# Contracting over 128 rows with zeros instead of 65 and 97, in the second layer's edge loop of a graph network on Trainium2

## The chip, the cores and the metric

The kernel runs on one core of one Trainium2 chip. The metric is the device time of one execution in microseconds (us); lower is better. Three executions of the kernel before are given, and one more was taken with the profiler, whose trace is what the rows below come from.

## What is computed

Two layers of an equivariant graph network on 12,500 nodes and 200,000 edges, each followed by a residual sum and a layer norm. The edges are sorted by their target node. Only the edge part of the second layer matters here. Its weights per edge come from a small two-stage network on 64 scalars of the edge, and end in a linear map to 224 numbers:

```python
w = h @ rw3 + roff                      # h: 64 numbers of an edge, w: 224
w1, w2, w3, w4, w5 = jnp.split(w, [C0, 2 * C0, 2 * C0 + C1, 2 * C0 + 2 * C1], axis=1)
o0a = w1 * ms                           # ms, mv: messages, gathered from source and target
o0b = w4 * (jnp.einsum('eud,ed->eu', mv, Y1) / SQ3)
o1a = (w2 * ms)[:, :, None] * Y1[:, None, :]
o1b = w3[:, :, None] * mv
o1c = w5[:, :, None] * (jnp.cross(mv, Y1[:, None, :]) / SQ2)
ds = jnp.concatenate([o0a, o0b], axis=1)        # 96 scalars
dv = jnp.concatenate([o1a, o1b, o1c], axis=1)   # 128 vectors
ls, lv = _eq_lin(ds, dv, lin_ws, lin_bs, lin_wv)
```

Attention logits, an exponential against the maximum of each target and sums by target follow.

## The kernel before

The program is written by hand, engine by engine, with semaphores. `layer1_edges` handles 1,568 tiles of 128 edges, four tiles at a time (`GT` = 4): 392 steps, in 49 passes of 8. One step does the following.

- GpSimd (POOL) first runs a one-element "settling" operation (L129, `e_gather_cell`) once `added` tells that a row buffer is free. Then it issues eight indirect DMAs (L1842), four that gather rows of the source table TS and four of the target table TD, into `rows`. There are two row buffers, so the gathers of a step may run beside the work on the step before.
- VectorE (DVE) adds the two gathered rows (L1854, in `sums`), forms dot and cross products, multiplies by the weights (L1878 to L1887, in `weigh`), and in `tail` finishes the previous step: product with the attention vector (L1897), the one-hot matrix q (L1904), a sum (L1909), a scaling (L1915), the logit (L1921). The queue's order is sums(next), weigh(next), tail(this one).
- TensorE (PE) multiplies the edge's 64 scalars, and a row of ones for the offset, by `w_r` (L1990, in `weights`, four matmuls of 65 rows x 224 columns; each stands in the trace as two records). It transposes the products (L2000, in `turn`, four rounds of four), sums by target for an earlier step (L2012, in `totals`, in two halves between the rounds), and maps the transposed products: scalars with `w_l` (L2024, 97 rows: 96 scalars and a one) and vectors with `w_lv` (L2026), both in `maps`. Its queue: weights(next), turn 0, turn 1, totals, turn 2, totals, turn 3, maps. In every fourth step a transpose of logits goes up (L2036) and one of maxima down (L2041), with scans on VectorE.
- ScalarE (ACT) copies the transposes out of PSUM (L2094, `keep`) and the totals (L2105), and takes the maps' result: silu (L2115) and a copy (L2120), in `results`. The silu waits for `mapped`, which the last matmul of L2026 updates. In every fourth step there is an exponential (L2079).
- The sync engine (SP) loads edge scalars (`e_h`, once the weight products that read the buffer are done), indices and rows, and stores the totals.

`weights2` loads the weights before: `load_weights` zeroes every tile on GpSimd and then fills it by DMA. Row 64 of `e_h` is set to one, once, before the loop (L1968), and column 96 of `e_ds` too (L1966); `ones_set` holds TensorE's first weight products until then.

Of the kernel before, what the change touches and what calls it, by code (L numbers as in the profile page):

```python
# [17 lines left out]
ACT = mybir.ActivationFunctionType  # L18
# [3 lines left out]
R = 128  # L22
NT, ET = 100, 1568
N, E = NT * R, ET * R
GT = 4
S, V = 64, 32
# [8 lines left out]
HEADS = 8  # L35
# [42 lines left out]
class Mem:  # L78
# [12 lines left out]
    def sb(self, name, shape, dt=F32):  # L91
        return self.ctx.enter_context(self.nc.sbuf_tensor(name, shape, dt))

    def sem(self, name):
        self.sems.append(self.nc.alloc_semaphore(name))
        return self.sems[-1]


def row_of(v, n):
    return v.rearrange("(a n) -> a n", a=1)[:, 0:n]  # L100


def col_of(v):
    return v.rearrange("(n a) -> n a", a=1)
# [8 lines left out]
def gate(eng, k):  # L113


    eng.wait_ge(k["ready"], 4)
# [781 lines left out]
def load_weights(nc, m, k, name, loads, also=()):  # L898

    done, zeroed = m.sem(name + "_loaded"), m.sem(name + "_zeroed")  # L900
    tiles = list(also)
    for tile, *_ in loads:
        if all(tile is not x for x in tiles):
            tiles.append(tile)
    with nc.Block() as block:
        @block.gpsimd
        def _(pool):
            for tile in tiles:
                pool.memset(tile[:], 0.0).then_inc(zeroed, 1)
            pool.wait_ge(zeroed, len(tiles))  # L910

        @block.sync
        def _(sp):
            sp.wait_ge(zeroed, len(tiles))
            for _, to, of in loads:
                sp.dma_start(to, of).then_inc(done, 16)
            sp.wait_ge(done, 16 * len(loads))


def scale_all(nc, m, k, name, scales):  # L920

    done = m.sem(name + "_scaled")
    with nc.Block() as block:
        @block.vector
        def _(dve):
            for ap, by in scales:
                dve.tensor_scalar(ap, ap, float(by), None, ALU.mult).then_inc(done, 1)
            dve.wait_ge(done, len(scales))
# [696 lines left out]
def weights2(nc, m, k, ps, w, W):  # L1625


    for n, shape in dict(r1=[128, 128], r2=[128, 128], avg=[128, 128], rb=[128, 8], r3=[S + 1, 224], l1=[97, 136],
                         lv=[128, V], ad=[128, S]).items():
        W[n] = m.sb("w_" + n, shape)  # L1630
    loads = []
    for h in range(2):
        lo = slice(S * h, S * h + S)
        loads += [(W["r1"], W["r1"][lo, lo], w["rw1"]), (W["r2"], W["r2"][lo, lo], w["rw2"])]
        for j, n in enumerate(("rb1", "rg1", "rbe1", "rb2", "rg2", "rbe2")):
            loads.append((W["rb"], W["rb"][lo, j:j + 1], col_of(w[n])))
    loads += [(W["r3"], W["r3"][0:S, :], w["rw3"]), (W["r3"], W["r3"][S:S + 1, :], row_of(w["roff"], 224)),
              (W["l1"], W["l1"][:], w["lin_by_head"]), (W["lv"], W["lv"][:], w["lin_wv"]),
              (W["ad"], W["ad"][:], w["alpha_dot"].rearrange("(a h) k -> a (h k)", a=1).broadcast_to([128, S]))]
    load_weights(nc, m, k, "w2", loads, [W["avg"]])  # L1640
    scale_all(nc, m, k, "w2", [(W["lv"][0:S], SQ3), (W["lv"][S + V:128], SQ3 / SQ2)])
    done, turned = m.sem("w2_done"), m.sem("w2_turned")
    mean = m.sb("w2_mean", [128, 8])
    tmp = m.sb("w2_tmp", [97, S])
    with nc.Block() as block:
        @block.vector
        def _(dve):
            n = 0

            def step(ins):  # L1650
                nonlocal n
                n += 1
                ins.then_inc(done, 1)
                dve.wait_ge(done, n)
            for h in range(2):
                lo = slice(S * h, S * h + S)
                step(dve.memset(W["avg"][lo, lo], 1.0 / S))
            for j, r in enumerate(("r1", "r2")):
                step(dve.tensor_reduce(mean[:, j:j + 1], W[r][:], AX.X, ALU.add))
                step(dve.tensor_scalar(mean[:, j:j + 1], mean[:, j:j + 1], 1.0 / S, None, ALU.mult))  # L1660
                for h in range(2):
                    lo = slice(S * h, S * h + S)
                    step(dve.tensor_scalar(W[r][lo, lo], W[r][lo, lo], mean[lo, j:j + 1], None, ALU.subtract))

            by_head = W["l1"][:].rearrange("u (h x) -> u h x", h=HEADS)
            t3 = tmp[:].rearrange("u (h k) -> u h k", h=HEADS)
            step(dve.tensor_tensor(t3, by_head[:, :, 0:8], W["ad"][0:97, :].rearrange("u (h k) -> u h k", h=HEADS), ALU.mult))
            step(dve.tensor_reduce(by_head[:, :, 8], t3, AX.X, ALU.add))
            step(dve.tensor_scalar(by_head[:, :, 8], by_head[:, :, 8], 0.2, None, ALU.mult))
            step(dve.tensor_scalar(W["ad"][:], W["ad"][:], 0.8, None, ALU.mult))  # L1670
            dve.wait_ge(turned, 1)
            step(dve.tensor_tensor(W["rb"][:, 0:6:3], W["rb"][:, 0:6:3], ps[:, 0, 0:6:3], ALU.subtract))

        @block.tensor
        def _(pe):
            pe.wait_ge(done, 2)
            pe.matmul(ps[:, 0, 0:6], W["avg"][:], W["rb"][:, 0:6], start=True, stop=True).then_inc(turned, 1)
            pe.wait_ge(turned, 1)
# [41 lines left out]
def layer1_edges(nc, m, k, ps, W, TS, TD, index, dstI, rows_dst, heads_dst, H, yx, TOT):  # L1720

    own = ExitStack()
    with own:
        mm = Mem(nc, own)
        sb, sem = mm.sb, mm.sem
        at = sb("e1_at", [R, 2, 2, 16], I32)
        row = sb("e1_row", [R, 2, 16 * R], I32)
        dh = sb("e1_dh", [128, 2, R], I32)
        hh = sb("e1_h", [65, 2, GT * R])
        rows = sb("e1_rows", [R, 2, 2, GT, X])  # L1730
        m_ = sb("e1_m", [R, 2, GT, X])
        prod, cA, cB, cr = (sb("e1_" + n, [R, GT, 3, V]) for n in ("prod", "cA", "cB", "cr"))
# [1 line left out]
        ds_, dv = sb("e1_ds", [R, 2, GT, 2, 128]), sb("e1_dv", [R, 2, GT, 3, 128])  # L1734
        dT = sb("e1_dT", [128, 4, GT * R])
# [10 lines left out]
        ones_set, added, crossed, mixed, w_ready, scaled, d_ready, turned, kept, mapped, outs = (sem("e1_" + n) for n in (  # L1746
            "ones_set", "added", "crossed", "mixed", "w_ready", "scaled", "d_ready", "turned", "kept", "mapped", "outs"))
# [9 lines left out]
        def head(c):  # L1757
            return out4[:, c, 0:8 * 29].rearrange("r (h x) -> r h x", x=29)
# [4 lines left out]
        with nc.Block() as block:  # L1763
# [83 lines left out]
            def _(dve):  # L1847
# [116 lines left out]
                        tail(i, True, not i.before(5))  # L1964

                dve.memset(ds_[:, :, :, 0, 96:97], 1.0)  # L1966
                dve.memset(mask[:], -BIG)
                dve.memset(hh[S:65], 1.0).then_inc(ones_set, 1)  # L1968
                dve.wait_ge(ones_set, 1)
                sums(At(0, 0))  # L1970
                weigh(At(0, 0))
                passes(dve, body)
# [6 lines left out]
            def _(pe):  # L1979
# [13 lines left out]
                def turn(i, j):  # L1993
                    p = i.r % 2
                    if not (i.before(1) and j < 2):
                        gate(pe, k)
                        pe.wait_ge(kept, i.n(4, j - 1))
                    for c in range(GT):
                        src = ds_[:, p, c, 0, 0:97] if j == 0 else dv[:, p, c, j - 1, :]
                        last = pe.transpose(ps[0:src.shape[1], 2 + j % 2, R * c:R * c + R], src, I[0:R, 0:R])  # L2000
                    last.then_inc(turned, 1)

# [13 lines left out]
                def maps(i):  # L2016
                    gate(pe, k)
                    pe.wait_ge(kept, i.n(4, 4))
                    if not i.before(1):
                        gate(pe, k)  # L2020
                        pe.wait_ge(outs, i.n(2))
                    for c in range(GT):
                        e = slice(R * c, R * c + R)
                        pe.matmul(head(c)[:, :, 0:17], dT[0:97, 0, e], W["l1"][:], start=True, stop=True)  # L2024
                        for x in range(3):
                            last = pe.matmul(head(c)[:, :, 17 + 4 * x:21 + 4 * x], dT[:, 1 + x, e], W["lv"][:],  # L2026
                                             start=True, stop=True)
                    last.then_inc(mapped, 1)
# [32 lines left out]
                        if r % 4 == 0 and not i.before(4):  # L2061
                            tops_down(i)

                pe.wait_ge(ones_set, 1)
                weights(At(0, 0))
                passes(pe, body)
                logits_up(At(PASSES, 0))
# [6 lines left out]
            def _(act):  # L2074
# [10 lines left out]
                                   ACT.Copy).then_inc(mkept, 1)  # L2085

                def keep(i, j):
                    wide = 97 if j == 0 else 128
                    gate(act, k)
                    act.wait_ge(turned, i.n(4, j + 1))  # L2090
                    if not i.before(1):
                        gate(act, k)
                        act.wait_ge(mapped, i.n(1))
                    act.activation(dT[0:wide, j, :], ps[0:wide, 2 + j % 2, :], ACT.Copy).then_inc(kept, 1)  # L2094

                def keep_totals(i, half):
                    j = i.r - 6
# [665 lines left out]
```

## Time and profile before

| | us |
|---|---|
| median of three runs (14,514.0 to 14,614.86) | 14,576.01 |
| the profiled execution | 14,720.34 |
| its span, first to last instruction | 14,718.6 |
| second layer's edges, of that span | about 6,422 |

The profiled execution is one more execution, 1.0% above the median. Busy time is what an engine's records cover. The granted clock is TensorE's, as a share of 2.4 GHz; its two levels are 1.0 and 0.5, and a value between them is a mean. PE is TensorE's matmuls and PEld its weight loads. "Idle before" in a row is how long the engine had been idle, with what is taken to have ended it; that is inferred, and where the named engine or transfer has nothing to do with the instruction the cause is another one.

### The profile page before, as it was taken

What the parts mean: (1) busy time and instruction counts of PE and PEld (TensorE: products, weight loads), DVE (VectorE), ACT (ScalarE), POOL (GpSimd) and SP (SyncE); (2) the same over time, 40 slices, a digit from 0 to 9 for tenths busy, and PEclk for the clock granted to TensorE, in tenths of its full rate; (3) what the DMA queues carried; (4) which work ended last, traced back from release to release, by engine and by line L of the source; (5) the groups of instructions that cost most, each with busy time, mean ns of one, the idle gap of its engine ahead of it and who ended that gap; (6) DMA issues with size and microseconds to landing.
All of it is one profiled execution on the core that took longest, in us unless ns stands there. A gap on an engine that the chain in (4) does not pass through costs nothing. (4 is left out here: it accounts for less than half of the span.)

```text
span 14718.6 us, 198660 instructions
## 1 busy us (share of the span) xinstructions
PE 11062.6 (75%) x42082; PEld 7618.9 (52%) x42082; DVE 8564.2 (58%) x16029; ACT 4894.4 (33%) x9080; POOL 8450.8 (57%) x7876
## 2 busy tenths in 40 slices
PE   0168888888879999967787878888788787853777
PEld 0034444444432222227777777777777777741444
DVE  6316666666659999975555555555555555532332
ACT  0026666666651111112232333333323333311333
POOL 0327888788779999975554555555555555534000
PEclk9959999999989999986666666666666666655555
DMA  2127777777779999962222322223322323221000
GB/s 113 39 101 151 154 154 154 152 156 154 154 146 218 218 220 219 219 147 77 86 86 84 89 88 88 87 85 90 89 85 88 89 86 90 89 61 39 13 13 13
DMA packets 1237597, 1650.64 MB, mean 112 GB/s; under 512 B 215337, under 2 KB 865917, under 8 KB 1207261
## 3 DMA queue, kind: packets, MB, share of 16 engines
q1 hardware_dynamic: 841700, 1188.34, 29.6%
q0 software_dynamic: 395520, 458.93, 17.8%
q14 instruction: 343, 2.80, 0.1%
q8 instruction: 34, 0.56, 0.0%
HBM read 1472.37 MB, written 443.97 MB: 130 GB/s over the span
## 5 line engine op out<-in xcount | busy, mean ns | idle before, releaser
L461 POOL DMA_INDIRECT sums<-e_total,e_place x1568 | 2483.3, 1584 | 460.1 <-issue 419.0
L1842 POOL DMA_INDIRECT e_rows<-TS,e_at x1568 | 1624.7, 1036 | 464.1 <-issue 420.9
L1842 POOL DMA_INDIRECT e_rows<-TD,e_at x1568 | 1511.0, 964 | 477.6 <-issue 477.6
L2012 PE MATMUL ps<-e_val,e_q 128*128 128x168 f32 x3136 | 1055.7, 488 | 828.0 <-DVE e_val L1915 516.6
L2026 PEld LDWEIGHTS ps<-w_lv,e_dT 128*128 128x128 f32 x9408 | 1571.9, 245 | 0.0
L2026 PE MATMUL ps<-w_lv,e_dT 128*128 128x32 f32 x9408 | 1525.4, 306 | 0.0
L1897 DVE TENSOR_TENSOR e_silu<-e_silu,w_ad 128x256 f32<-128x256 f32 x392 | 166.6, 425 | 2315.2 <-ACT e_val L2120 1971.3
L598 PE MATMUL ps<-e_win,e_pick 128*128 128x448 f32 x3136 | 1348.4, 576 | 204.4 <-DVE e_u L495 152.9
L129 POOL TENSOR_TENSOR e_gather_cell<-zeros 1x1 f32<-1x1 f32 x392 | 186.2, 475 | 2244.4 <-DVE e_m L1854 2114.6
L2012 PEld LDWEIGHTS ps<-e_val,e_q 128*128 128x128 f32 x3136 | 803.2, 314 | 973.7 <-issue 932.3
L1990 PE MATMUL ps<-w_r,e_h 65*128 65x224 f32 x3136 | 1149.7, 537 | 129.0 <-issue 59.8
L1111 POOL TENSOR_TENSOR n_zv<-n_zv 128x512 f32<-128x512 f32 x400 | 1197.5, 2994 | 37.2 <-POOL n_zv L1111 0.9
L2115 ACT ACTIVATE e_silu<-ps 128x256 f32<-128x256 f32 x392 | 150.2, 383 | 3051.9 <-DMA e_win<-T 2389.4
L2024 PE MATMUL ps<-w_l,e_dT 97*128 97x136 f32 x3136 | 920.3, 382 | 312.7 <-ACT e_dT L2094 185.0
L2094 ACT ACTIVATE e_dT<-ps 128x512 f32<-128x512 f32 (+1 forms) x1568 | 913.6, 598 | 666.6 <-PE ps L2000 537.5
L2000 PE MATMUL ps<-ident,e_dv 128*128 128x128 f32 x4704 | 1111.9, 383 | 30.9 <-issue 20.0
L598 PEld LDWEIGHTS ps<-e_win,e_pick 128*128 128x128 f32 x3136 | 621.5, 204 | 970.3 <-issue 876.8
L1990 PEld LDWEIGHTS ps<-w_r,e_h 65*128 65x128 f32 x3136 | 893.2, 299 | 207.0 <-issue 136.1
L2000 PEld LDWEIGHTS ps<-ident,e_dv 128*128 128x128 f32 x4704 | 927.3, 209 | 69.7 <-issue 36.5
L129 POOL TENSOR_TENSOR e_pool_cell<-zeros 1x1 f32<-1x1 f32 x1568 | 810.6, 517 | 239.6 <-DVE e_place L554 154.6
L1281 PE MATMUL ps<-n_z,w_uss 128*64 128x512 f32 x1600 | 762.9, 621 | 116.8 <-DVE n_z L1130 115.7
L2024 PEld LDWEIGHTS ps<-w_l,e_dT 97*128 97x128 f32 x3136 | 588.0, 233 | 429.7 <-issue 392.6
(392 smaller groups left out, 21971.2 us busy)
## 6 DMA issues: line engine op xcount, KB each, us to landing
e_win<-T SPq DMA_DIRECT2D x1568, 168.0 KB
n_z<-in_x_columns SPq DMA_DIRECT2D x400, 512.0 KB
n_zv<-in_x_columns SPq DMA_DIRECT2D x800, 192.0 KB
TOT<-e_tot SPq DMA_DIRECT2D x392, 352.0 KB
e_row<-in_src_rows SPq DMA_DIRECT2D x98, 1024.0 KB
e_row<-in_dst_rows SPq DMA_DIRECT2D x98, 1024.0 KB
e_win<-T SPq DMA_DIRECT2D x1568, 56.0 KB
e_local<-LR SPq DMA_DIRECT2D x98, 512.0 KB
```

The lines of the kernel that those rows point to most:

```text
L129: pool.tensor_tensor(self.cell[:], z, z, ALU.add).then_inc(self.done, 1)
L461: pool.indirect_dma_start(sums[c], bass.IndirectOffsetOnAxis(ap=place[:, p, c:c + 1], axis=0), total[:, p, c, 0:MSG0], None, compute_op=AL ...
L598: pe.matmul(g[:, c, :], pick[:, p, R * c:R * c + R], win[:, s, c, :], start=True, stop=True).then_inc(spread, 1)
L1111: pool.tensor_tensor(zv[:, b, 0], zv[:, b, 0], zv[:, b, i], ALU.add).then_inc(zv_ready, 1)
L1281: last = pe.matmul(ps[0:S, U0, :], W["uss"][:, 4 * s + j, :], z[:, s % 4, j, :], start=False, stop=False)
L1842: pool.indirect_dma_start(rows[:, p, x, c, :], None, table, bass.IndirectOffsetOnAxis(ap=at[:, gp, x, col:col + 1], axis=0)).then_inc(rows ...
L1990: last = pe.matmul(w4[:, c, 0:224], hh[:, p, R * c:R * c + R], W["r3"][:], start=True, stop=True)
L2000: last = pe.transpose(ps[0:src.shape[1], 2 + j % 2, R * c:R * c + R], src, I[0:R, 0:R])
L2012: last = pe.matmul(tot2[:, c % 2], q[:, j % 2, c, :], val[:, slot // 4, 4 * (slot % 4) + c, :], start=True, stop=True)
L2024: pe.matmul(head(c)[:, :, 0:17], dT[0:97, 0, e], W["l1"][:], start=True, stop=True)
L2026: last = pe.matmul(head(c)[:, :, 17 + 4 * x:21 + 4 * x], dT[:, 1 + x, e], W["lv"][:], start=True, stop=True)
L2094: act.activation(dT[0:wide, j, :], ps[0:wide, 2 + j % 2, :], ACT.Copy).then_inc(kept, 1)
```

## The change

The weight products and the scalars' map contract over all 128 rows. The rows that were not there are zeros: in `w_r` and `w_l` from the zeroing of the tiles, in `e_h` from a memset before the loop, in `e_ds` (columns 97 to 127) likewise. Since the transpose of `e_ds` now takes 128 columns, ScalarE copies 128 partitions. Both parts are in one diff:

```diff
-    for n, shape in dict(r1=[128, 128], r2=[128, 128], avg=[128, 128], rb=[128, 8], r3=[S + 1, 224], l1=[97, 136],
+    for n, shape in dict(r1=[128, 128], r2=[128, 128], avg=[128, 128], rb=[128, 8], r3=[128, 224], l1=[128, 136],
-              (W["l1"], W["l1"][:], w["lin_by_head"]), (W["lv"], W["lv"][:], w["lin_wv"]),
+              (W["l1"], W["l1"][0:97, :], w["lin_by_head"]), (W["lv"], W["lv"][:], w["lin_wv"]),
-            by_head = W["l1"][:].rearrange("u (h x) -> u h x", h=HEADS)
+            by_head = W["l1"][0:97, :].rearrange("u (h x) -> u h x", h=HEADS)
-        hh = sb("e1_h", [65, 2, GT * R])
+        hh = sb("e1_h", [128, 2, GT * R])
                 dve.memset(ds_[:, :, :, 0, 96:97], 1.0)
+                dve.memset(ds_[:, :, :, 0, 97:128], 0.0)
                 dve.memset(mask[:], -BIG)
+                dve.memset(hh[S:128], 0.0).then_inc(ones_set, 1)
+                dve.wait_ge(ones_set, 1)
                 dve.memset(hh[S:65], 1.0).then_inc(ones_set, 1)
-                dve.wait_ge(ones_set, 1)
+                dve.wait_ge(ones_set, 2)
-                        src = ds_[:, p, c, 0, 0:97] if j == 0 else dv[:, p, c, j - 1, :]
+                        src = ds_[:, p, c, 0, :] if j == 0 else dv[:, p, c, j - 1, :]
-                        pe.matmul(head(c)[:, :, 0:17], dT[0:97, 0, e], W["l1"][:], start=True, stop=True)
+                        pe.matmul(head(c)[:, :, 0:17], dT[:, 0, e], W["l1"][:], start=True, stop=True)
-                pe.wait_ge(ones_set, 1)
+                pe.wait_ge(ones_set, 2)
-                    wide = 97 if j == 0 else 128
-                    act.activation(dT[0:wide, j, :], ps[0:wide, 2 + j % 2, :], ACT.Copy).then_inc(kept, 1)
+                    act.activation(dT[:, j, :], ps[:, 2 + j % 2, :], ACT.Copy).then_inc(kept, 1)
```

The matmul of the weight products, `pe.matmul(w4[:, c, 0:224], hh[:, p, ...], W["r3"][:])`, is the same line before and after; its rows follow from the tiles.

## Rows read from the trace of the kernel before

**Rows 1.** Window of the stage: PE, PEld, DVE, ACT, POOL busy; clock, DMA share, GB/s.
```profile
6590.00:13012.00 6422.00, 5186.99 (x25116) 4772.00 (x25117) 3383.22 (x7505) 1934.78 (x3497) 3312.10 (x3517) 0.64 0.29 87
```

**Rows 2.** Timeline of one step, by engine: start, length, what, idle before.
```profile
9979.82 0.52 POOL L129 TENSOR_TENSOR e_gather_cell<-zeros 1x1 f32<-1x1 f32 x1 [4.11 <-DVE e_m L1854]
...
9990.01 0.94 POOL L1842 DMA_INDIRECT e_rows<-TD,e_at  x1 [0.30 <-issue]
...
9980.99 0.85 PE L2012 MATMUL ps<-e_val,e_q 128*128 128x168 f32 x4
...
9983.04 0.49 PE L2024 MATMUL ps<-w_l,e_dT 97*128 97x136 f32 x2 [0.62 <-issue]
...
9986.08 0.75 PE L2026 MATMUL ps<-w_lv,e_dT 128*128 128x32 f32 x6
...
9986.82 1.68 PE L1990 MATMUL ps<-w_r,e_h 65*128 65x224 f32 x8
...
9995.47 1.48 PE L2012 MATMUL ps<-e_val,e_q 128*128 128x168 f32 x4 [5.92 <-issue]
...
10000.59 0.82 PE L2024 MATMUL ps<-w_l,e_dT 97*128 97x136 f32 x2 [0.76 <-issue]
...
9992.15 0.38 ACT L2115 ACTIVATE e_silu<-ps 128x256 f32<-128x256 f32 x1 [9.24 <-DMA e_win<-T]
...
9978.77 0.82 DVE L1854 TENSOR_TENSOR e_m<-e_rows 128x640 f32<-128x640 f32 x1
...
9995.32 0.81 DVE L1854 TENSOR_TENSOR e_m<-e_rows 128x640 f32<-128x640 f32 x1
```

**Rows 3.** Windows in that step, TensorE alone: busy, granted clock, DMA share, GB/s.
```profile
9981.00:9983.00 2.00, 1.42 (x10) 0.96 0.14 41
...
9989.00:9991.00 2.00, 0.53 (x4) 1.00 0.32 81
...
9993.00:9995.00 2.00, 0.00 (x0) 0.50 0.00 0
```

**Rows 4.** Waits of the stage: engine, line, for whom; us in total, times, longest.
```profile
ACT e_silu L2115 <- DMA e_win<-T: 2389.4, 294, 11.2
...
ACT e_silu L2115 <- PE ps L2026: 587.3, 82, 8.4
```

**Rows 5.** Timeline and window of a step mostly at the low clock.
```profile
9032.23 0.79 PE L2024 MATMUL ps<-w_l,e_dT 97*128 97x136 f32 x2
9032.81 1.33 PE L2026 MATMUL ps<-w_lv,e_dT 128*128 128x32 f32 x6
9033.95 3.33 PE L1990 MATMUL ps<-w_r,e_h 65*128 65x224 f32 x8
...
9024.29 0.81 DVE L1854 TENSOR_TENSOR e_m<-e_rows 128x640 f32<-128x640 f32 x1
9040.77 0.81 DVE L1854 TENSOR_TENSOR e_m<-e_rows 128x640 f32<-128x640 f32 x1
...
9033.95:9037.08 3.13, 3.13 (x9) 0.50 0.20 61
```

**Rows 6.** Durations by line: shortest, median, longest ns, of 65 rows and of 128.
```profile
L1337 PE MATMUL ps<-w_msd,n_ns x200: 275/302/553, 4547.3 to 6527.7; 65*128 65x128 f32 x100
...
L2000 PE MATMUL ps<-ident,e_dv x4704: 269/421/476, 6599.7 to 13028.2; 128*128 128x128 f32 x196
...
L2000 PE MATMUL ps<-ident,e_ds x1568: 269/421/521, 6598.9 to 13021.6; 128*97 128x128 f32 x196
```

**Rows 7.** ScalarE's copies of the transposes, by form: busy, mean ns, idle before.
```profile
L2094 ACT ACTIVATE e_dT<-ps 128x512 f32<-128x512 f32 x1176 | 703.1, 598 | 311.0 <-PE ps L2000 213.6 <-issue 57.9 <-DMA e_win<-T 37.3
...
L2094 ACT ACTIVATE e_dT<-ps 97x512 f32<-97x512 f32 x392 | 233.8, 596 | 355.6 <-PE ps L2000 323.9 <-issue 17.4 <-DMA e_win<-T 13.8
```

**Rows 8.** Timeline of VectorE where the stage begins.
```profile
6575.81 0.91 DVE L1968 MEMSET e_h<- 1x1024 f32 x1 [0.25 <-issue]
6589.31 0.83 DVE L1854 TENSOR_TENSOR e_m<-e_rows 128x640 f32<-128x640 f32 x1 [12.59 <-DMA e_rows<-TD,e_at]
```

## The prediction

> **What bounds the kernel now.** I began with the window of the one stage that the change touches, the edges of the second layer, some 6,422 us of the 14,718.6 us span [rows 1]. TensorE is busy for 5,187 us of it (81%), VectorE for 53%, GpSimd for 52%, and the granted clock is 0.64 on average, so TensorE spends most of this stage at the lower of its two levels, 1.2 GHz. Read alone, this says that TensorE bounds the stage and that its clock is what to raise. The timeline of one step says otherwise.
>
> The stage runs 392 steps. VectorE's L1854 starts each one: 391 intervals between 6589.3 and 13013.4 us give 16.43 us a step. In the step of [rows 2], from 9978.77 to 9995.32 us (16.55 us), the clock was at 2.4 GHz from 9981 to 9991 us [rows 3]. The maps (L2024, L2026) ran from 9983.04 to 9986.83, the weight products (L1990) to 9988.5, the first transposes (L2000) to 9989.55. Then TensorE stood idle for 5.92 us. What everything waited for is ScalarE's silu (L2115), which needs nothing but the maps' result. It started at 9992.15, that is 5.3 us after the last record of the maps. After it the order is fixed: VectorE's tail, L1854 3.17 us later, and then GpSimd's settling operation and the next eight gathers (L1842). The gathers' issuing ends at 9990.95, 11.1 us after the settling operation began at 9979.82, and the DMA share, 0.32 up to 9991 us, is nothing from 9993 us on [rows 2, 3]: the silu starts about when the gathers' traffic ends.
>
> So a step is a ring: 1.05 us from L1854 to the settling operation, 12.33 us of gathers from there to the silu, 3.17 us of silu and tail to the next L1854, 16.55 us together. The mean step is 16.43. Why the end of the maps reaches ScalarE only with the end of the gathers the records don't say; that it does so in most steps the list of waits says. ScalarE's wait before the silu is put down to the maps in 82 steps only, 587 us, and in 294 steps, 2,389 us, to a DMA that has nothing to do with it, which means that the maps' last record was long over [rows 4].
>
> The step of [rows 5] is the check. Most of its TensorE work ran at 1.2 GHz (8 records of L1990 took 3.33 us against 1.68 us in [rows 2]), and from L1854 to L1854 it took 16.48 us. One step with the high clock in its heavy part and one with the low clock are the same length to 0.07 us.
>
> **The change part by part.** (1) The weight products contract over 128 rows, not 65. Instructions, columns and passes are the same: 3,136 matmuls, 3,136 weight loads. The nearest pair of rows: a product of 65 rows and 128 columns took 275 ns at its shortest, a transpose of 128 rows and 128 columns 269 ns [rows 6]. Rows cost nothing; taken whole, the difference is -6 ns x 3,136 = -19 us, and it lies beside the idle time of [rows 2]. I take 0, bounds -19 and 0.
>
> (2) The scalars' map goes from 97 rows to 128, and the transposes that feed it take 128 columns of `e_ds` as their weights, not 97. Both forms have the same shortest and median matmul, 269 and 421 ns [rows 6]. 0 us.
>
> (3) ScalarE keeps 128 partitions, not 97: 598 against 596 ns [rows 7], 392 times, +0.8 us if it were all on the path.
>
> (4) Two memsets once: 64 partitions x 1,024 elements of `e_h`, as long as L1968's 0.91 us, 248 elements of `e_ds`, a quarter of that, and one wait more [rows 8]. VectorE waits 12.59 us for the first gather right behind them, so they are covered there; TensorE's first products wait for them too, but nothing needs these before L1854's sums. Without that cover: +1.3 us, which I count.
>
> (5) Zeroing and loading the wider weight tiles adds partitions, no elements to a partition. 0 us. No step is moved past a queue, no DMA is added.
>
> (6) The clock is the one effect that can be large. In [rows 5] L1990 kept TensorE busy without a gap from 9033.95 to 9037.08, all at 0.50; in [rows 2, 3] the clock had risen by about 9981 us, behind totals (L2012), which contract over 128 rows. So being busy is not all that counts; work on 65 rows seems to count less. Nothing shows that zeros count like data. The Trainium skill ("TensorE: Matmul & The Clock Gate", What's actually happening) says that the gate follows how busy the engine has recently been. By that rule the zero rows change nothing, since no busy time changes, and the sum stays at +2 us; the trace disagrees in that L1990 fills the engine and the clock stays low.
>
> If the clock does rise, its worth is read from the ring. Maps at 1.2 GHz take (1.33 - 0.75) + (0.79 - 0.49) = 0.88 us longer for each of four tiles [rows 5]; the shorter ones are those of [rows 2], so 3.5 us. Where the silu waits for the gathers' end, this is worth 0: that wait is next. Only in the 82 steps where the maps ended it can something be won, at most 3.5 us each (-287 us), at least 0. I take 0.2 us x 82 = -16 us, near the low end, since once the maps are earlier the gathers' end decides these steps as well, and [rows 2] against [rows 5] shows no difference.
>
> Sum: -16 + 0.8 + 1.3 = -14 us on the profiled execution of 14,720 us. The median of the runs shown is 14,576, 1.0% below it; scaled, 14,562 us.
>
> **The rivals.** *The ring is more TensorE's than I read (A).* If the waits put down to a DMA hide a slow TensorE, a higher clock shortens every step. At 0.5 to 1.0 us a step, 392 steps: -200 to -390 us, 14,190 to 14,380. For it: TensorE busy 81%, clock 0.64. Against it: 5.92 us of idle at the high clock.
>
> *The late result is a matter of rows (B).* The maps and the products are the only matmuls here on fewer than 128 rows, and the result that comes late is theirs. If full rows let the silu start when the maps end, it starts 5.3 us earlier; then silu to maps is 8.4 us (9992.15 to 10000.59, [rows 2]) and maps 3.8 to 7.3 us, 12.2 to 15.7 us a step, above GpSimd's own 11 us. That is -0.8 to -4.3 us in the 310 steps whose silu starts late: 13,240 to 14,330. Against it: the silu follows the gathers' end and not a count of rows. Nothing excludes it.
>
> *The clock at the wrong time (C), slower.* Zeros raise the clock in the weight products; those end early, TensorE idles, the clock falls, and totals, transposes and maps, which lie on the way to the silu, run at 1.2 GHz. That way is 8.4 + 7.3 = 15.7 us against the ring's 16.5, a slack of 0.8 us. It decides when anything takes up these 0.8 us (a step in which the row group's scans are made). At 0.2 to 0.6 us on the 310 steps that don't wait for the maps now: +60 to +190 us, 14,640 to 14,760.
>
> *The change doesn't do what it says (D):* the zeros don't count for the clock. 14,578 us; its time is the forecast's.
>
> **How the numbers follow.** Forecast with D: 0.64, own range 14,480 to 14,640. A 0.12, B 0.11, C 0.13. The predicted time is 14,562. The range goes from 14,250 to 14,760: it takes in the forecast, C and half of A, and leaves out B nearly whole and the rest of A, some 0.17. A difference under 1% (146 us) can't be told from none by a measurement of this kernel. A and B are faster by more, with a little of the forecast's edge: 0.24. A third of C and a small part of what I can't name are slower by more: 0.09. The rest is 0.67.
>
> **What the changed profile would show.** L1990 as 128*128 128x224 and L2024 as 128*128 128x136 with unchanged shortest records; L2094 in one form. If zeros count, the stage's granted clock rises from 0.64 to 0.75 or so and the busy time of TensorE falls by some hundreds of us, while its idle time before L2012 grows by the same: the step stays at 16.4 us. If they don't, 0.64 stays. Under A the step and TensorE's busy time fall together. Under B the silu starts within some 0.05 us of the last L2026 while gathers are still being issued. Under C the maps' records get longer. The forecast is wrong if the step's mean moves by more than 0.4 us; the step of my argument that would then be wrong is that the gathers' end and not TensorE lets the silu start.

## The result, and the profile after

| | before | after |
|---|---|---|
| median of four runs, same chip, us | 14,587.03 | 14,412.86 |
| lowest to highest, us | 14,514.0 to 14,614.86 | 14,372.71 to 14,460.3 |
| profiled execution, span, us | 14,718.6 | 14,458.5 |

The ratio is 0.9893, with a 95% interval of 0.9862 to 0.9924: 1.1% faster. The medians differ by 174 us and the spans of the profiled executions by 260 us; the second layer's edge stage has all of it: from its first L1854 to its last it took 6,424 us before and 6,142 us after, 16.43 and 15.71 us a step. The profiled execution before, 14,720.34 us, is above the highest of the four timed ones, so what follows from this pair of traces may overstate the change by up to 90 us. In the profile after, the lines behind the first memset are numbered 1 to 3 higher.

The window of the stage, with the columns of [rows 1]:

```profile
6610.00:12752.00 6142.00, 4705.58 (x25122) 4307.07 (x25122) 3381.41 (x7507) 1916.04 (x3499) 3330.68 (x3518) 0.74 0.31 91
```

The granted clock rose from 0.64 to 0.74 and TensorE's busy time fell by 481 us, on the same instructions. But the stage is only 280 us shorter: the rest turned into idle time. The costliest groups of the page after:

```profile
L2015 PE MATMUL ps<-e_val,e_q 128*128 128x168 f32 x3136 | 871.8, 416 | 899.8 <-DVE e_val L1915 418.7
...
L129 POOL TENSOR_TENSOR e_gather_cell<-zeros 1x1 f32<-1x1 f32 x392 | 181.0, 462 | 1946.5 <-DVE e_m L1854 1823.7
L2096 ACT ACTIVATE e_dT<-ps 128x512 f32<-128x512 f32 x1568 | 901.8, 597 | 983.9 <-PE ps L2003 542.0
...
L2027 PE MATMUL ps<-w_l,e_dT 128*128 128x136 f32 x3136 | 918.1, 382 | 330.5 <-ACT e_dT L2096 218.4
L1993 PE MATMUL ps<-w_r,e_h 128*128 128x224 f32 x3136 | 1049.9, 501 | 125.6 <-issue 56.2
```

A product took 501 ns on average, 537 before; the scalars' map 382 both times; the totals, which were not touched, 416 against 488. By line (shortest, median and longest ns), the rows themselves cost nothing:

```profile
L1993 PE MATMUL ps<-w_r,e_h x3136: 352/581/743, 6599.4 to 12749.1; 128*128 128x224 f32 x196
```

With 65 rows the same record is 349/581/743. The waits of the stage after, against [rows 4]:

```profile
ACT e_silu L2117 <- DMA e_win<-T: 1724.6, 229, 11.5
ACT e_silu L2117 <- PE ps L2029: 727.5, 116, 8.3
```

The silu's waits that are put down to a foreign DMA went from 294 to 229. They mark a maps' result that comes late, by about 1.5 us or more: measured from the maps' last record, 287 of 374 steps before and 232 after are that late. One step after in which it came early, by the timeline:

```profile
9949.56 0.81 DVE L1854 TENSOR_TENSOR e_m<-e_rows 128x640 f32<-128x640 f32 x1
...
9950.60 0.53 POOL L129 TENSOR_TENSOR e_gather_cell<-zeros 1x1 f32<-1x1 f32 x1 [5.68 <-DVE e_m L1854]
...
9957.16 0.75 PE L2029 MATMUL ps<-w_lv,e_dT 128*128 128x32 f32 x6
9957.74 1.76 PE L1993 MATMUL ps<-w_r,e_h 128*128 128x224 f32 x8
9958.08 0.95 POOL L1842 DMA_INDIRECT e_rows<-TD,e_at  x1 [0.30 <-issue]
9958.48 0.38 ACT L2117 ACTIVATE e_silu<-ps 128x256 f32<-128x256 f32 x1 [4.49 <-PE ps L2029]
...
9960.58 0.95 POOL L1842 DMA_INDIRECT e_rows<-TD,e_at  x1 [0.31 <-issue]
9961.65 0.82 DVE L1854 TENSOR_TENSOR e_m<-e_rows 128x640 f32<-128x640 f32 x1
```

The maps end at 9957.91 and the silu starts 0.57 us later, with two gathers still to be issued: 12.09 us from L1854 to L1854, where the step of [rows 2] took 16.55.

To see all steps at once I took from the instruction records, for each of 374 steps (the stage's first and last ones left out), the start of the settling operation, the end of the last L2026/L2029 record, and the starts of the silu and of L1854. Means in us:

```
                        before  after   from
step                    16.42   15.69   L1854 to the next L1854
L1854 to settling        1.05    1.10
settling to maps' end    8.72    8.70   last record of the maps
maps' end to silu        3.11    2.32   "delay" below
silu to L1854            3.54    3.57
silus over 12 us after
the settling operation    220     120   of 374
delays under 0.3 us        39      85   of 374
```

So the maps end no earlier, counted from the settling operation. The gain of 0.73 us is the shorter delay between the maps' end and the silu, 0.79 us; the small rest goes the other way.

### The profile page after: what moved, and what is told of

It is laid out like the page before. It is cut to its first block and busy times, and to the rows that moved or that the text cites. A ratio compares the mean times of both kernels' runs of the same rounds, so it can differ in the third digit from the quotient of the medians.

```text
span 14458.5 us, 198662 instructions
## 1 busy us (share of the span) xinstructions
PE 10587.8 (73%) x42082; PEld 7153.9 (49%) x42082; DVE 8553.3 (59%) x16031; ACT 4875.3 (34%) x9080; POOL 8466.1 (59%) x7876
## 5 line engine op out<-in xcount | busy, mean ns | idle before, releaser
L2029 PEld LDWEIGHTS ps<-w_lv,e_dT 128*128 128x128 f32 x9408 | 1538.5, 241 | 0.0
L2015 PE MATMUL ps<-e_val,e_q 128*128 128x168 f32 x3136 | 871.8, 416 | 899.8 <-DVE e_val L1915 418.7
L2029 PE MATMUL ps<-w_lv,e_dT 128*128 128x32 f32 x9408 | 1492.2, 302 | 0.0
L2096 ACT ACTIVATE e_dT<-ps 128x512 f32<-128x512 f32 x1568 | 901.8, 597 | 983.9 <-PE ps L2003 542.0
L2015 PEld LDWEIGHTS ps<-e_val,e_q 128*128 128x128 f32 x3136 | 645.5, 257 | 1041.7 <-issue 917.0
L2027 PE MATMUL ps<-w_l,e_dT 128*128 128x136 f32 x3136 | 918.1, 382 | 330.5 <-ACT e_dT L2096 218.4
L1993 PE MATMUL ps<-w_r,e_h 128*128 128x224 f32 x3136 | 1049.9, 501 | 125.6 <-issue 56.2
L2003 PE MATMUL ps<-ident,e_dv 128*128 128x128 f32 x4704 | 931.9, 334 | 143.0 <-ACT e_dT L2096 74.2
L1993 PEld LDWEIGHTS ps<-w_r,e_h 128*128 128x128 f32 x3136 | 827.2, 277 | 186.1 <-issue 79.1
L2003 PEld LDWEIGHTS ps<-ident,e_dv 128*128 128x128 f32 x4704 | 767.0, 179 | 183.7 <-issue 93.7
L2027 PEld LDWEIGHTS ps<-w_l,e_dT 128*128 128x128 f32 x3136 | 588.0, 234 | 442.8 <-issue 406.8
```

What stands on the lines that cost most here:

```text
L1993: last = pe.matmul(w4[:, c, 0:224], hh[:, p, R * c:R * c + R], W["r3"][:], start=True, stop=True)
L2015: last = pe.matmul(tot2[:, c % 2], q[:, j % 2, c, :], val[:, slot // 4, 4 * (slot % 4) + c, :], start=True, stop=True)
L2027: pe.matmul(head(c)[:, :, 0:17], dT[:, 0, e], W["l1"][:], start=True, stop=True)
L2096: act.activation(dT[:, j, :], ps[:, 2 + j % 2, :], ACT.Copy).then_inc(kept, 1)
```

## The experiments

Each was timed against the kernel before on its own chip. The kernel before took 14,755.79 us beside the first four, 14,770.71 beside the next four, 12,845.04 beside the three after those, and 14,526.28 beside the last. The third figure is a finding of its own (below).

### Which part carries it

**e1**, the weight products alone at 128 rows:

```diff
-... r3=[S + 1, 224], l1=[97, 136],
+... r3=[128, 224], l1=[97, 136],
-        hh = sb("e1_h", [65, 2, GT * R])
+        hh = sb("e1_h", [128, 2, GT * R])
+                dve.memset(hh[S:128], 0.0).then_inc(ones_set, 1)
```

> Only the weight products contract over 128 rows; the scalars' map keeps 97. Theory K (the zero rows count for the clock, and the higher clock shortens the steps in which TensorE's way to the silu decides): the products are the long run of work on few rows, so nearly the whole gain is here, 0.8 to 1.1% faster, stage clock 0.64 to about 0.72. Theory L (the late arrival of the maps' result at ScalarE is a matter of the maps' own rows): the map still has 97 rows, so no gain, within 0.3%.

14,557.34 us, ratio 0.9860 (0.9838 to 0.9883); step 16.01 us, delay 2.57.

**e2**, the scalars' map alone:

```diff
-                        pe.matmul(head(c)[:, :, 0:17], dT[0:97, 0, e], W["l1"][:], start=True, stop=True)
+                        pe.matmul(head(c)[:, :, 0:17], dT[:, 0, e], W["l1"][:], start=True, stop=True)
```

with the transposes and ScalarE's copies at 128 as in the change.

> Only the scalars' map contracts over 128 rows, with transposes and copies to match; the products keep 65. Theory K: 97 to 128 rows in 8 of 32 short matmuls is little, 0 to 0.3% faster, stage clock within 0.03 of 0.64. Theory L: the whole gain, about 1.1%, and more steps in which the silu starts within 0.3 us of the maps' last record.

14,741.84 us, ratio 0.9987 (0.9977 to 0.9996); step 16.42 us, delay 3.31.

**e3**, products at 96 rows:

```diff
+... r3=[96, 224], ...
+        hh = sb("e1_h", [96, 2, GT * R])
```

> The weight products contract over 96 rows, filled with zeros; the map keeps 97. Theory K: half of the way from 65 to 128 rows, so clock and time lie between, 0.2 to 0.8% faster, stage clock 0.66 to 0.71. If zeros count only for the clock when the array is full: as before, within 0.2%.

14,603.52 us, ratio 0.9899 (0.9884 to 0.9914); step 16.05 us, delay 2.82. The products carry the gain, the map gives next to nothing, and 31 rows of zeros already give most of it. Both gains are above what theory K had put on them (0.8 to 1.1% for e1, 0.2 to 0.8% for e3). That full rows in the map let its own result through falls with e2.

### Is it the clock?

**e4**, rows as before, four fillers ahead of each step's products:

```diff
                     for c in range(GT):
+                        pe.matmul(w4[:, c, 0:128], I[:], I[:], start=True, stop=True)
+                    for c in range(GT):
                         last = pe.matmul(w4[:, c, 0:224], hh[:, p, R * c:R * c + R], W["r3"][:], ...
```

> Rows as before (65 and 97), but four added matmuls of the identity with itself, 128 rows by 128 columns, ahead of each step's weight products, into the same PSUM columns, which the products then overwrite. They add 0.4 to 0.9 us of TensorE work to each step. Theory K: what matters is the clock and not the operands' own rows, so stage clock at 0.70 or more and 0.5 to 1.5% faster. Theory L: the same rows, so no gain, 0 to 1% slower.

14,732.35 us, ratio 0.9985 (0.9976 to 0.9995). That is neither theory K's gain nor theory L's loss. The windows of the stage of e2 and of e4:

```profile
6600.00:13010.00 6410.00, 4876.61 (x25046) 4486.40 (x25046) 3375.25 (x7488) 1922.37 (x3483) 3316.52 (x3524) 0.69 0.30 87
```

```profile
6600.00:13000.00 6400.00, 5426.87 (x28249) 5028.23 (x28250) 3390.76 (x7509) 1939.26 (x3495) 3313.54 (x3528) 0.70 0.30 87
```

Those of e1 and of e3:

```profile
6600.00:12900.00 6300.00, 4996.26 (x25142) 4565.34 (x25143) 3398.79 (x7524) 1916.66 (x3501) 3335.76 (x3528) 0.70 0.31 89
```

```profile
6600.00:12880.00 6280.00, 4973.45 (x25066) 4549.00 (x25066) 3374.80 (x7489) 1911.18 (x3486) 3328.81 (x3528) 0.69 0.31 89
```

e2 and e4 have the clock of e1 (0.70) and e3 (0.69), and neither has their gain. e2 is the plainest case: 310 us less of TensorE's busy time than before, and no step shorter. The records tell where in the step the clock was high, by the share of a line's records that start at a granted clock of 1.0: in e1 and e3 in about half of the totals (0.61 and 0.46 of their records, 0.51 in the changed kernel), in e2 in 0.11 of them, 0.09 before. e4 speaks against this reading too: it has the high clock in 0.40 of them, and its step is 16.33 us, its delay 2.87. The next two kernels put fillers where TensorE waits for the totals' input.

**e7** on the kernel before and **e8** on the changed one:

```diff
+                    if half == 0:
+                        for c in range(6):
+                            pe.matmul(tot2[:, c % 2, 0:128], I[:], I[:], start=True, stop=True)
                     gate(pe, k)
                     pe.wait_ge(u_ready, i.n(1, 1, 6))
```

with the wait for `totkept` moved ahead of them.

> The kernel before, rows 65 and 97, with six more matmuls of 128 rows by 128 columns (identity by identity, into the bank of the totals, written over at once) put ahead of each step's first totals, in the place where TensorE waits for the tail: 1.6 us at the high clock, 2.5 us at the low one. Theory W (what counts is in which part of the step the clock is high: on the way from the silu to the maps' end, totals and transposes, where the changed kernel has it in 51 to 58% of their records and the kernel before in 9 to 25%): the clock is up in totals and the later transposes in over half of the steps, the step falls from 16.4 to 15.6 to 15.9 us though no row was added, the run is 1.0 to 2.0% faster than the kernel before. Theory Z (the gain comes from the rows of the products themselves and not from the clock, which four fillers ahead of the products had already raised to 0.70 in the stage for 0.15%): within 0.3% of the kernel before, or slower by what the fillers take, up to 1% more.

> The changed kernel (128 rows in both) with the same six fillers ahead of each step's first totals. Theory W: the clock is up in nearly all of the totals and later transposes; the step falls by some 0.3 to 0.6 us more, from 15.7 to 15.1 to 15.4 us, and the ratio to the kernel before is 0.975 to 0.985 (the changed kernel has 0.989). Theory Z: no better than the changed kernel, 0.987 to 1.0, since the fillers only take time where the tail is early.

e7: 14,798.57 us, ratio 1.0007 (0.9989 to 1.0024). e8: 14,676.08 us, ratio 0.9942 (0.9923 to 0.9962), worse than the change without fillers. Windows of e7, then of e8:

```profile
6611.00:13150.00 6539.00, 5566.39 (x29730) 5196.47 (x29731) 3385.62 (x7508) 1927.44 (x3498) 3325.86 (x3517) 0.71 0.29 85
```

```profile
6608.00:12936.00 6328.00, 5040.87 (x29728) 4651.74 (x29729) 3383.29 (x7507) 1911.43 (x3498) 3314.57 (x3516) 0.80 0.30 88
```

In e7 the totals had the high clock in 0.83 of their records, and the step was 16.73 us. That theory, W, fell as well: in e7 the fillers pushed the maps' end out (9.50 us after the settling operation, 8.72 before). But the delay of e7 was 2.54 us, as short as e1's, on 65 and 97 rows: it takes no row of zeros to shorten it, and here the later maps used up the gain. In e8 they were not later (8.64), and yet the delay was 2.90 us against 2.32 of the change. More clock, the same maps' end, a longer delay: the clock's mean is not what the time follows.

### What holds the silu

**e5** leaves out the four gathers of the target table (the second row buffer is a constant 0.5); **e6** leaves GpSimd's gathers out altogether, and the sync engine loads as many bytes, always the same 512 rows of each table:

```diff
-                            for c in range(GT):
+                            for c in range(GT if x == 0 else 0):
```

```diff
+                    for x, table in enumerate((TS, TD)):
+                        sp.dma_start(rows[:, p, x], table[0:GT * R].rearrange("(r c) x -> r c x", c=GT)
+                                     ).then_inc(rows_here[p][x], 16)
```

> Leaves out the four gathers of the target table in each step: the second row buffer is set to 0.5 once, so the sums are made with a constant. Everything else is the kernel before, rows 65 and 97. Theory G (the silu is let go by the gathers' traffic, as the prediction has it): settling operation to silu falls from a mean of 11.9 us to 6 to 8 us, because half of the gathers are gone; the silu then starts at the maps' end or soon after, and the step falls from 16.4 us to what TensorE needs, 13 to 14 us; the run gives 13,300 to 13,900 us. Theory T (the way of TensorE from the silu over tail, weights, transposes and totals to the maps' end sets the step, gathers or not): that way is 15 to 16 us at the low clock, so the step stays at 15.5 us or more and the run gives 14,250 us or more.

> Takes GpSimd's indirect gathers out of the loop: the sync engine loads two blocks of 512 rows of the tables with plain transfers instead, as many bytes, always the same rows; so the messages are those of other nodes. Rows 65 and 97 as in the kernel before. Theory G' (what holds back the maps' result is the gathers that GpSimd issues): the silu starts within 0.3 us of the last record of the maps in nearly all steps, where the kernel before has 11% of such steps and a mean of 3.1 us; the step falls to TensorE's own way, 12 to 14 us, and the run to 12,900 to 13,800 us. Theory G'' (it is the traffic on the rows' path as such, whoever starts it): the delay stays above 1.5 us in most steps and ends with the transfers.

e5: 12,992.94 us, ratio 0.8795 (0.8782 to 0.8807), step 11.98 us, delay 0.40. e6: 12,822.43 us, ratio 0.8684 (0.8671 to 0.8696), step 11.53 us, delay 0.06. e5 came below the times of theory G (a step of 13 to 14 us, 13,300 us or more), e6 just below those of G' (12,900 us or more). The silu's waits in e5, then in e6 (four more, put down to the maps too, stand under the line alone):

```profile
ACT e_silu L2116 <- PE ps L2027: 1400.9, 351, 7.3
ACT e_silu L2116 <- DMA e_win<-T: 194.2, 33, 6.5
```

```profile
ACT e_silu L2106 <- PE ps L2017: 1411.5, 386, 5.5
```

294 late waits before, 33 with half of the gathers, none without GpSimd's. The times of the semaphore updates say the same for every signal of TensorE. In the kernel before, the updates of the stage whose matmul's record ended in the first 4 us after a settling operation came 13 ns behind the record in 99 of 100 cases (1,298 updates). Where the record ended 5 to 12 us after it, 98 of 100 came late (860 updates, by up to 7.3 us), half of them 12.3 us after the settling operation. Where it ended 14 to 20 us after, none of 351 did. (Pairs more than 9 us apart, where a record is missing from the trace, are left out.) In e6, 95 of 100 updates of each of the stage's four signals come within 14 ns, and this beside full traffic: in the step whose maps end at 9002.35 and whose silu starts at 9002.39, the share of the DMA engines was

```profile
9001.00:9002.00 1.00, 1.00 (x11) 1.00 (x10) 0.46 (x2) 0.00 (x0) 0.00 (x0) 1.00 1.03 392
```

The other engines' signals are not late: in the stage of the kernel before, none of VectorE's 3,415 updates and of ScalarE's 2,886 came more than 30 ns behind a record. What exactly in the gathers holds TensorE's signal, GpSimd's issuing or the scattered rows that are in flight, these two runs don't tell apart; e6 takes both away at once. A step of e5:

```profile
9009.73 0.52 POOL L129 TENSOR_TENSOR e_gather_cell<-zeros 1x1 f32<-1x1 f32 x1 [4.89 <-DVE e_m L1853]
...
9014.19 1.47 POOL L1842 DMA_INDIRECT e_rows<-TS,e_at  x1 [0.30 <-issue]
...
9015.18 0.75 PE L2027 MATMUL ps<-w_lv,e_dT 128*128 128x32 f32 x6
9016.35 0.38 ACT L2116 ACTIVATE e_silu<-ps 128x256 f32<-128x256 f32 x1 [4.34 <-PE ps L2027]
```

The maps end at 9015.93 and the silu starts at 9016.35, 6.62 us after the settling operation; of 187 steps of e5 whose maps end 6 to 7 us after it, 8 in 10 have their silu between 6.5 and 6.7 us. With four gathers that is the commonest time, with eight 12.3 us.

### Mending the delay

**e9** tests whether what TensorE runs behind the maps matters; **e10** (rows as before) and **e11** (128 rows) hold the second four gathers back until the maps have ended:

```diff
+                    if not i.before(2):
+                        gate(pe, k)
+                        pe.wait_ge(outs, i.n(2, 1, 2))
                     for c in range(GT):
                         last = pe.matmul(w4[:, c, 0:224], ...
```

```diff
                         for x, table in enumerate((TS, TD)):
+                            if x == 1:
+                                if not i.before(3):
+                                    gate(pool, k)
+                                    pool.wait_ge(mapped, i.n(1, 1, 3))
+                                settle_td(pool, i.n(1))
                             for c in range(GT):
```

> The kernel before, rows 65 and 97, with one wait more: the weight products that follow the maps on TensorE wait until the silu of the same step has started and ended, so TensorE does nothing between the maps' end and the silu. In the runs so far, among steps whose maps end 6.4 to 8.2 us after the settling operation, the silu came 9.4 to 10.3 us after it where the products ran at 1.2 GHz behind the maps, and 10.6 to 12.0 us where they ran at 2.4 GHz. Theory S (what TensorE runs behind the maps decides how long their signal is held back): with nothing behind them the silu comes within 1 to 2 us of the maps' end in most steps, the step falls by 0.5 to 2 us if the later products do not cost more, and the run is 1 to 4% faster. Theory N (TensorE's own work has nothing to do with it, only the gathers in flight): the mean delay from the maps' end to the silu stays at 2.5 us or more; the products then start later, the way to the next maps is 1 to 3 us longer, and the run is 1 to 5% slower.

> The kernel before, rows 65 and 97, with GpSimd's eight gathers of a step split: the four of the source table go out as before, the four of the target table wait until the maps of the step at hand have ended (a wait and a second settling operation on GpSimd). All gathers are still made, and each step's rows are read one step later. Theory H (TensorE's signals pass while up to four gathers are in flight and are held from about 4.5 us after the settling operation to the end of the eighth gather at 12.3 us): with four gathers only, as in the run without the target table's gathers, the silu comes 6.5 to 7.5 us after the settling operation, with a delay under 0.5 us; the step falls to 12.5 to 14 us, bounded by GpSimd's 11 us of issuing and its wait, and the run gives 13,100 to 13,800 us, 7 to 11% faster. Theory N2 (the delay has nothing to do with the number of gathers in flight): the delay stays, the gathers end later, and the run is slower than before.

> The same split of the gathers in the changed kernel, with 128 rows in both. Theory H: with the signal no longer held, the step is TensorE's and GpSimd's; the split alone raises the clock since TensorE idles less, so the rows add little: within 1% of the split with 65 and 97 rows, either side, and 7 to 11% below the kernel before. If the changed kernel's gain came from the clock as such, it should be kept on top: 1% or more below the split with 65 and 97 rows.

e9: 13,455.58 us, ratio 1.0473 (1.0455 to 1.0490). e10: 12,846.75 us, 1.0000 (0.9991 to 1.0010). e11: 12,807.01 us, 0.9961 (0.9947 to 0.9975). These ran on a chip where the kernel before takes 12,845 us, and there the delay isn't: 0.06 us in all three. The silu's waits of e9:

```profile
ACT e_silu L2118 <- PE ps L2029: 1426.1, 371, 7.3
ACT e_silu L2118 <- issue: 57.0, 15, 4.0
```

e9 keeps the eight gathers as the kernel before has them, and no wait is put down to a DMA. So the late signal belongs to these kernels on some chips only, or at some times: no chip was used for two sets of runs, so the chip and its state at the time can't be told apart. What e9 and e10 were to tell could not be told there; what e9 shows is only the price of products that start late, 4.7%. Two things can be read all the same. Outside the stage the chips are alike: span less stage is 8,294 us for the kernel before on the first, 8,326 us for e10 here. And e11 against e10, the change where nothing is late, is 12,807.01 to 12,846.75: 0.3% faster (the intervals reach 0.1% to either side). The window of e10's stage:

```profile
6623.00:11140.00 4517.00, 3850.62 (x25122) 3547.48 (x25122) 3382.29 (x7508) 1939.77 (x3499) 3642.28 (x3908) 0.89 0.43 123
```

With the signals on time, 65 and 97 rows get a clock of 0.89, since the work is packed into 11.55 us a step.

**e12** is e11 once more:

> The changed kernel with the split gathers once more, for a chip on which the kernel before takes about 14,770 us; the last call's chip ran the kernel before in 12,845 us with every signal of TensorE on time, so the split had nothing to mend there (ratio 1.0000 with 65 and 97 rows). Theory H (signals held while more than four gathers are in flight): on a chip of the 14,770 us kind the split gives a step of 11.5 to 13.5 us and a run of 12,800 to 13,600 us, ratio 0.87 to 0.92, with delays under 0.5 us in most steps. Theory N2 (the number of gathers in flight doesn't matter, any gather holds the signals): the delay stays, since the second four gathers now run over the start of the next step; 14,300 us or more. On a chip of the 12,845 us kind both expect 12,807 us again, and the question stays open.

Its chip was of the other kind: the kernel before 14,526.28 us, e12 13,693.32 us, ratio 0.9412 (0.9384 to 0.9439), the fastest of all versions that do the whole work on such a chip; the change alone gave 0.9893. Window, the silu's waits, and the timeline of two steps:

```profile
6618.00:11979.00 5361.00, 4470.73 (x25122) 4134.05 (x25122) 3390.56 (x7508) 1933.66 (x3499) 3490.34 (x3907) 0.78 0.36 104
```

```profile
ACT e_silu L2123 <- PE ps L2035: 1717.4, 332, 7.3
ACT e_silu L2123 <- DMA e_win<-T: 299.5, 50, 9.0
```

```profile
9047.57 0.18 POOL L129 TENSOR_TENSOR e_gather_cell<-zeros 1x1 f32<-1x1 f32 x1
...
9052.67 1.33 PE L2035 MATMUL ps<-w_lv,e_dT 128*128 128x32 f32 x6
9054.09 0.39 ACT L2123 ACTIVATE e_silu<-ps 128x256 f32<-128x256 f32 x1 [4.73 <-PE ps L2035]
9054.19 0.18 POOL L129 TENSOR_TENSOR e_gather_td_cell<-zeros 1x1 f32<-1x1 f32 x1 [1.17 <-issue]
9054.86 0.97 POOL L1848 DMA_INDIRECT e_rows<-TD,e_at  x1 [0.48 <-issue]
...
9060.86 0.55 POOL L129 TENSOR_TENSOR e_gather_cell<-zeros 1x1 f32<-1x1 f32 x1 [1.27 <-DVE e_m L1860]
```

The silu comes 6.52 us after the settling operation (mean 7.48, no step over 12), with a delay of 0.09 us here and 0.49 on average; 50 late waits are left of 294. Theory H's mechanism held and its price did not: I expected a ratio of 0.87 to 0.92. The split with 65 and 97 rows was not timed on such a chip, so how much of the 5.9% is the split's own is not shown. The step is 13.70 us, and of it 2.69 us (1.05 before) pass from L1854 to the settling operation, since GpSimd is still issuing the second four gathers; these now also hold the signals of the next step's transposes: of the updates for the transposes of `e_dv` that fall into the first 2 us after a settling operation some 60 to 80 in 100 are late, at most 5 in 100 in the kernel before.

## Why the prediction was right or wrong

**The time.** 14,562 was forecast, 14,412.86 came, inside the range of 14,250 to 14,760 but below the forecast's own cases (14,480 to 14,640): faster by just over 1%, which had a chance of 0.24. The step's mean moved by 0.72 us, so by the prediction's own test (0.4 us) the forecast is wrong. The range holds the result only because it was drawn wide enough to take in half of rival A; for the forecast's mechanism that is luck.

**The terms that were right.** Rows cost no time on TensorE (352 against 349 ns shortest, equal medians). ScalarE's copy took 597 ns. The memsets stayed under VectorE's wait for the first gather, which went from 12.59 to 11.30 us, that is 1.3 us, as counted:

```profile
6597.07 0.91 DVE L1969 MEMSET e_h<- 64x1024 f32 x1 [0.25 <-issue]
6598.25 0.91 DVE L1971 MEMSET e_h<- 1x1024 f32 x1 [0.27 <-DVE e_h L1969]
6610.46 0.83 DVE L1854 TENSOR_TENSOR e_m<-e_rows 128x640 f32<-128x640 f32 x1 [11.30 <-DMA e_rows<-TD,e_at]
```

Zeros count for the clock: 0.64 became 0.74 (0.75 was written), and TensorE's busy time fell by hundreds of us. A shorter step may raise the clock too; e2, whose step stayed at 16.42 us, went to 0.69. The Trainium skill ("TensorE: Matmul & The Clock Gate", What's actually happening) ties the clock to how busy the engine is. The traces disagree, if busy means that a matmul is running: e2 has the matmuls of the kernel before in the same order and as many, with zeros added in the map and in the transposes that feed it, and a higher clock at the same step. And the kernel before has steps in which TensorE is busy without a gap and the clock stays low, with work on 65, 97 and 128 rows among it (TensorE alone):

```profile
12355.70:12370.40 14.70, 14.70 (x60) 0.50 0.25 72
```

Of the 481 us that TensorE's busy time fell by, 200 came back as idle time.

**The term that failed.** It is the worth of the clock's rise, part (6): -16 us, from "worth 0" in the steps where the silu waits for the gathers' end. The stage measured -282 us in the two traces; in the timed runs the whole change is worth -174 us. The step behind it, that the gathers' end and not TensorE lets the silu start, holds for what e5 and e6 show: it is GpSimd's gathers in flight that hold the signal, and with them gone the run is 1,948 us shorter. It fails as a fixed time: in 154 of 374 steps before and in 254 after the silu starts less than 12 us after the settling operation, in 72 and 174 of them before the last gather is issued. I had two steps, both near 16.5 us, and took them for all. They were no test of the clock either: in the one of [rows 5] the first three of the four tiles' maps, on the way to its silu, ran at the high clock too:

```profile
9029.50:9032.60 3.10, 3.10 (x26) 0.94 0.78 215
```

All 374 steps of the same trace speak against it: 5 in 100 are under 14.2 us and 10 in 100 over 19.1, and the ring's 12.33 us from settling operation to silu is the commonest value, not the only one. The count of 82 steps "where the maps ended it" was off as well: in 39 of 374 steps only was the delay under 0.3 us; in 48 more it was 0.3 to 1.5 us, a late signal too.

**The rivals.** A has the nearest size: 0.72 us a step in the traces, inside its 0.5 to 1.0 us, though the median is some 30 us above its 14,190 to 14,380. Its reason is only half right: busy time and step did fall together, but e2 and e4 raise the clock and shorten the step by 0.1 us at most, and e7 lengthens it. B, a matter of rows, falls with the change itself, whose delay is 2.32 us with full rows everywhere. C, the clock at the wrong time, falls too: the totals had the high clock in 0.51 of their records, 0.09 before, and the scalars' map took 382 ns as before. e7 and e8 share with it that more clock bought nothing, not the mechanism. D falls with the clock.

**What stays open.** Why the delay is shorter with 128 rows in the products. In the steps (scans' steps left out) whose maps end 6.4 to 8.2 us after the settling operation and beside which the sync engine's queue moved nothing, the silu starts on average

```
clock from 8 to 11 us after settling     low             high
before                                    -              11.97 (35 steps)
after                                    9.35 (53)       10.57 (77)
e1                                      10.23 (101)       -
e2                                        -              11.56 (100)
e3                                      10.17 (73)       11.93 (17)
e4                                      10.15 (35)       11.45 (28)
e7                                      10.35 (75)       10.80 (4)
e8                                      10.20 (21)       11.55 (35)
```

us after it. In each of the five kernels that have both, the signal gets out earlier where TensorE runs the products behind it at the low clock; and the kernel before has no such step, the change has 53, e2, with none, gained nothing. That is a pattern, not a cause, and it has gaps: at the high clock the change is 1.4 us earlier than the kernel before, which the clock behind the maps can't explain; and counting the steps with sync-engine traffic too, the kernel before has 4 at the low clock, whose silu comes at 11.60 us, no earlier than the rest. e9 was made for it and its chip had no delay. Nor is it settled whether the signal or the maps' last write is late: the Trainium skill ("Perfetto Trace Analysis", Tensor Engine Instruction (MATMUL, LD_WEIGHTS)) says that a matmul's recorded end is an estimate and that its update follows the acknowledgement of its writes. By that the writes themselves may be held while gathers are in flight; no run here tells the two apart.

## What to carry to other kernels

Look at all repetitions of a step before you call it a ring with a fixed term: two steps of equal length stood here for a spread of 14 to 19 us. And compare them where it counts: both had most of their maps at the high clock. When a consumer's wait is put down to a transfer that it has nothing to do with, its real producer's signal is late; find out what is in flight at that time and move that, which gave 5.9% with the change where the change alone gave 1.1%. And time on more than one chip: what is worth 5.9% on one (e12) was worth 0.4% on another (e11, the same program).

## What the runs showed that I had not expected

- On the chips where the kernel before takes 14,500 to 14,800 us, TensorE's semaphore updates come up to 7 us late while GpSimd's indirect gathers are in flight (98 of 100 between 5 and 12 us after the settling operation); VectorE's and ScalarE's don't, and plain transfers of as many bytes don't do it (95 of 100 within 14 ns).
- On another chip the same program takes 12,845 us. In three kernels traced there, one with its gathers as before, the delay is 0.06 us in the mean. It is as long as e6 takes on a chip of the first kind, 12,822 us.
- Rows of zeros raise the granted clock: 65 rows 0.64, 96 rows 0.69, 128 rows 0.70 (e1), at equal instructions. In e1 and e3 the shorter step may add to it; in e2 (the map alone, 0.69) the step was as before.
